# Routed experts on one core: row gathers in eight groups between GpSimd's weight splits, and the first tile's low part before the second split on VectorE

## The chip, the cores and the metric

The kernel runs on one core of a Trainium2 chip. A core has five engines that run side by side and meet only in semaphores: TensorE (PE), VectorE (DVE), ScalarE (ACT), GpSimd (POOL) and SyncE (SP), which here only issues DMAs. The metric is the device time of one execution in microseconds (us), as the median of several runs.

## The reference, cut to what matters

The program is two layers: cross attention and a gated feed-forward, then a state-space mixer and a mixture of experts. The change is in the mixture of experts alone, on 2048 tokens of 512 numbers, 16 experts, two for each token:

```python
logits = xt @ Wr.T + bias                      # 2048 x 16
probs = jax.nn.softmax(logits, axis=-1)
topk_val, topk_idx = jax.lax.top_k(probs, 2)
g = jnp.einsum('th,ehi->tei', xt, Wg)          # Wg, Wu: 16 x 512 x 256
u = jnp.einsum('th,ehi->tei', xt, Wu)
y = jnp.einsum('tei,eih->teh', jax.nn.silu(g) * u, Wd)   # Wd: 16 x 256 x 512
routed = jnp.einsum('tke,tk,teh->th', oh, w, y)
```

With these inputs and this routing the experts get 183, 203, 191, 89, 465, 257, 221, 103, 104, 332, 487, 937, 45, 11, 36 and 432 token slots.

## The kernel before, in words

The stages run one after the other; the last three are the router, the experts (`stage_experts`) and the sum (`stage_combine`). The router sorts the 4096 token slots by expert, and each expert's slots are padded to whole tiles of 128 rows. The number of tiles is fixed at 47 (`TILES`). From the counts above the experts 0 to 15 own 2, 2, 2, 1, 4, 3, 2, 1, 1, 3, 4, 8, 1, 1, 1 and 4 tiles, 40 in all; the seven tiles behind them are padding and use the last expert's weights. So tile 6 is the only one of expert 3, tiles 7 to 10 are expert 4's, 11 to 13 expert 5's, 14 and 15 expert 6's, tile 16 is expert 7's, tile 17 expert 8's, tiles 18 to 20 are expert 9's, 21 to 24 expert 10's, 25 to 32 expert 11's, and tile 35 is expert 14's.

`stage_experts` works a tile at a time. PE turns the tile's rows (`exp_x`, L2528), multiplies them with the expert's gate and up weights (`exp_g`), turns the hidden rows (`exp_h`) and multiplies them with the down weights (`exp_y_ps`). Every product is done in three passes with operands split in a high part (the fp32 number rounded by the cast) and a low part (the rest), `split_product`, L96. So the weights of an expert must be split before they can be used, and the tile's turned rows too: ACT writes their high part (`x_hi`, L2456), DVE their low part (`x_lo`, L2500).

Who does what, in which order:

- **SP** loads the raw weights of expert e: gate and up (`exp_raw`, two buffers, L2410) as soon as expert e-2 has been split, down (`exp_raw_down`, one buffer, L2413) as soon as expert e-1 has been split.
- **DVE** splits the weights of experts 0, 1 and 2 first (L2493, L2495), all three in a row, and only then takes the low part of tile 0's rows. Then it runs the loop over tiles.
- **POOL** first issues all 47 row gathers (L2421), one indirect DMA of 128 rows of 2 KB for each tile, in seven groups of 4, 4, 8, 8, 8, 8 and 7. A group has a semaphore of its own; after the issue of group g it waits for the landing of group g-1 and adds its size to `s_rows`. Behind the last gather it waits for the last group too. Only then does it split the weights of experts 3 to 15, one after the other (L2436, L2439: four instructions for an expert). Three experts' split weights fit (`WRING` is 3), so the split of expert e also waits until PE has done the last tile of expert e-3 (the wait on `s_y`).
- **ACT** copies a tile's gathered rows into a small buffer (`fetch`, L2451) two tiles ahead, when `s_rows` says that they are there. In its queue the copy for tile k+2 stands ahead of tile k's silu (L2474).
- **PE** waits before tile k's gate and up product for the split weights of its expert (`s_w`) and for the low part of the tile's rows (`s_xlo`).

Of the kernel before, what the change touches and what calls it, by code (L numbers as in the profile page):

```python
# [29 lines left out]
class Steps:  # L30
# [13 lines left out]
    def wait_apart(self, pace):  # L44
        wait_apart(self.eng, self.sem, self.base + self.n, pace)
# [1385 lines left out]
EXPERTS = 16  # L1431
# [585 lines left out]
WRING = 3  # L2017
# [320 lines left out]
def stage_experts(nc, xn, y, Wg, Wu, Wd, ident, plan):  # L2338
# [3 lines left out]
    IC = INNER // P  # L2342
    N_IN = KD * 2 * INNER
    N_ALL = N_IN + IC * DIM
    GROUPS = [4, 4] + [8] * 4 + [7]
    assert sum(GROUPS) == TILES
    with Scope(nc, "exp") as m:
        ident_sb = m.sb("ident", [P, P])
# [14 lines left out]
        s_raw, s_rawd = [m.sem(f"raw_in{i}") for i in range(2)], m.sem("raw_down_in")  # L2363
        s_gather = [m.sem(f"gathered{g}") for g in range(len(GROUPS))]
        s_rows = m.sem("rows_in")
# [12 lines left out]
        def pieces(e):  # L2378

            return ((raw[e % 2], slice(0, N_IN), s_raw[e % 2], 32 * (e // 2 + 1)),  # L2380
                    (raw_d, slice(N_IN, N_ALL), s_rawd, 16 * (e + 1)))
# [4 lines left out]
        def tiles(eng, step):  # L2386


            step(0, 0)
            pairs = (TILES - 3) // 2  # L2390
            with eng.Fori(0, pairs) as pair:
                step(pair * 2 + 1, 1)
                step(pair * 2 + 2, 0)
            for k in range(2 * pairs + 1, TILES + 1):
                step(k, k % 2)

        def known(k, test):

            return test(k) if isinstance(k, int) else True

        with m.block() as block:
            @block.sync
            def _(sp):
                sp.dma_start(ident_sb[:, :], ident).then_inc(s_id, 16)
                for e in range(EXPERTS):
                    if e >= 2:
                        sp.wait_ge(s_w, e - 1)
                    wi = raw[e % 2][:, 0:N_IN].rearrange("p (k g n) -> p k g n", k=KD, g=2)
                    for g, src in enumerate((Wg, Wu)):
                        sp.dma_start(wi[:, :, g, :], src[e].rearrange("(k p) n -> p k n", p=P)).then_inc(s_raw[e % 2], 16)  # L2410
                    if e:
                        sp.wait_ge(s_w, e)
                    sp.dma_start(raw_d[:, :].rearrange("p (k n) -> p k n", k=IC),  # L2413
                                 Wd[e].rearrange("(k p) n -> p k n", p=P)).then_inc(s_rawd, 16)

            @block.gpsimd
            def _(pool):
                k = 0
                for g, size in enumerate(GROUPS):
                    for _ in range(size):  # L2420
                        pool.indirect_dma_start(rows[:, k, :], None, xn,  # L2421
                                                bass.IndirectOffsetOnAxis(plan.source[:, k:k + 1], 0)
                                                ).then_inc(s_gather[g], 16)
                        k += 1
                    if g:
                        pool.wait_ge(s_gather[g - 1], 16 * GROUPS[g - 1])
                        pool.sem_inc(s_rows, GROUPS[g - 1])
                pool.wait_ge(s_gather[-1], 16 * GROUPS[-1])
                pool.sem_inc(s_rows, GROUPS[-1])
                for e in range(WRING, EXPERTS):  # L2430
                    end = pool.value_load(plan.ends[0:1, e - WRING:e - WRING + 1], min_val=0, max_val=TILES)
                    wait_apart(pool, s_y, end + 2, s_pace)
                    pool.wait_ge(s_w, e)
                    for n, (src, cols, sem, value) in enumerate(pieces(e)):
                        pool.wait_ge(sem, value)
                        pool.tensor_scalar(w[:, e % WRING, 0, cols], src[:, :], 1.0, 1.0, ALU.mult,  # L2436
                                           ALU.mult).then_inc(s_hi, 1)
                        pool.wait_ge(s_hi, 2 * (e - WRING) + n + 1)
                        pool.tensor_tensor(w[:, e % WRING, 1, cols], src[:, :], w[:, e % WRING, 0, cols].bitcast(F32),  # L2439
                                           ALU.subtract).then_inc(s_w if n else s_wpart, 1)  # L2440
                    pool.wait_ge(s_wpart, e + 1)

            @block.scalar
            def _(act):
# [40 lines left out]
            @block.vector  # L2485
            def _(dve):
                dve.sem_inc(s_xlo, 2)
                dve.sem_inc(s_h, 2)
                dve.sem_inc(s_hlo, 2)
                for e in range(WRING):  # L2490
                    for n, (src, cols, sem, value) in enumerate(pieces(e)):
                        dve.wait_ge(sem, value)
                        dve.tensor_copy(w[:, e, 0, cols], src[:, :]).then_inc(s_split, 1)  # L2493
                        dve.wait_ge(s_split, 2 * e + n + 1)
                        dve.tensor_tensor(w[:, e, 1, cols], src[:, :], w[:, e, 0, cols].bitcast(F32),  # L2495
                                          ALU.subtract).then_inc(s_w if n else s_wpart, 1)

                def x_lo(k, i):
                    dve.wait_ge(s_xhi, k + 1)
                    dve.tensor_tensor(xT[i][:, 1, :, :], ps_x[i][:, :, :], xT[i][:, 0, :, :].bitcast(F32),  # L2500
                                      ALU.subtract).then_inc(s_xlo, 1)

                x_lo(0, 0)

                def step(k, i):
                    if known(k, lambda k: k >= 1):
                        dve.wait_ge(s_hhi, k)
                        dve.tensor_tensor(hT[1 - i][:, 1, :, :], ps_h[1 - i][:, :, :], hT[1 - i][:, 0, :, :].bitcast(F32),
                                          ALU.subtract).then_inc(s_hlo, 1)
                    if known(k, lambda k: k + 1 < TILES):  # L2510
                        x_lo(k + 1, 1 - i)
                    if known(k, lambda k: k < TILES):
                        dve.wait_ge(s_silu, k + 1)
                        dve.tensor_tensor(hid[i][:, :], ps_g[i][:, 1, :], hid[i][:, :], ALU.mult).then_inc(s_h, 1)

                tiles(dve, step)
# [97 lines left out]
def build(nc, x, ctx_1024, L0_xattn_Wq, L0_xattn_Wk, L0_xattn_Wv, L0_xattn_Wo, L0_xattn_gq, L0_xattn_gk,  # L2614
# [20 lines left out]
    with Memory(nc, "residual") as r:  # L2635
# [14 lines left out]
        with Memory(nc, "normed2") as n:  # L2650
            normT2 = [n.sb(f"b{b}", [P, 2, KD, S], F32R) for b in range(B)]
            stage_norm(nc, "nrm2", xs, normT2, ident, rowsout=xrows)
            stage_shared_router(nc, xs, mixed, normT2, L1_ffn_sWg, L1_ffn_sWu, L1_ffn_sWd, L1_ffn_Wr, L1_ffn_bias, ident, iota, before, token, plan)

    stage_experts(nc, xrows, slots, L1_ffn_Wg, L1_ffn_Wu, L1_ffn_Wd, ident, plan)
    stage_combine(nc, mixed, slots, result, plan)
    decided.close()
# [30 lines left out]
```

## Time and profile before

| what | us |
| --- | --- |
| median of 3 runs (2758.46 to 2761.99) | 2759.77 |
| the profiled execution, its own time | 2749.03 |
| its span, first to last instruction | 2747.2 |
| stage of the experts in it, first gather to last product, about | 2371.5 to 2687 |

The profiled execution is one run on its own and was 10.7 us faster than the median of the three; its span leaves out 1.8 us around the instructions. Times in the trace count from the start of the span. The stage of the experts is 316 us of it.

### The profile page before, as it was taken

What the parts mean: (1) busy time and instruction counts of PE and PEld (TensorE: products, weight loads), DVE (VectorE), ACT (ScalarE), POOL (GpSimd) and SP (SyncE); (2) the same over time, 40 slices, a digit from 0 to 9 for tenths busy, and PEclk for the clock granted to TensorE, in tenths of its full rate; (3) what the DMA queues carried; (4) which work ended last, traced back from release to release, by engine and by line L of the source; (5) the groups of instructions that cost most, each with busy time, mean ns of one, the idle gap of its engine ahead of it and who ended that gap; (6) DMA issues with size and microseconds to landing.
All of it is one profiled execution on the core that took longest, in us unless ns stands there. A gap on an engine that the chain in (4) does not pass through costs nothing. (4 is left out here: it accounts for less than half of the span.)

```text
span 2747.2 us, 37910 instructions
## 1 busy us (share of the span) xinstructions
PE 2310.0 (84%) x10784; PEld 1774.8 (65%) x10785; DVE 1898.2 (69%) x3625; ACT 1235.3 (45%) x2129; POOL 1361.7 (50%) x1722
## 2 busy tenths in 40 slices
PE   3699999999999999998784898998998839459980
PEld 2687888878787878887533665665665426447770
DVE  6576777767677767776675989999999876412223
ACT  2353444544444444454483655655655412024440
POOL 0233333333243333332384888878988803478324
PEclk7799999999999999999886999999999958679995
DMA  7512232122322232220457555464665220565317
GB/s 276 206 62 101 85 109 86 62 90 85 109 85 76 76 109 85 85 77 28 142 202 237 176 180 184 173 197 151 205 195 158 86 89 16 201 201 175 130 54 256
DMA packets 136939, 363.84 MB, mean 132 GB/s; under 512 B 21280, under 2 KB 58912, under 8 KB 118560
## 3 DMA queue, kind: packets, MB, share of 16 engines
q1 hardware_dynamic: 123648, 328.36, 35.5%
q0 software_dynamic: 6320, 20.71, 2.4%
q10 hardware_dynamic: 6768, 12.32, 1.2%
q8 instruction: 94, 1.54, 0.2%
q14 instruction: 109, 0.89, 0.1%
HBM read 290.06 MB, written 71.30 MB: 132 GB/s over the span
## 5 line engine op out<-in xcount | busy, mean ns | idle before, releaser
L662 POOL TENSOR_SCALAR att_probs<-att_probs,att_recip 128x512 f32<-128x512 f32 x256 | 183.9, 722 | 402.5 <-DVE att_recip L743 398.1
L1837 POOL TENSOR_TENSOR mix_drive<-mix_du,mix_rows 128x512 f32<-128x512 f32 x256 | 326.5, 1282 | 61.4 <-DMA mix_rows<-bc_d 29.1
L585 ACT ACTIVATE att_probs<-att_s,att_bias,att_rq 128x512 f32<-128x512 f32 x256 | 199.9, 781 | 301.3 <-DVE att_bias L739 299.1
L1890 DVE TENSOR_TENSOR_SCAN mix_state<-mix_state,mix_drive 128x512 f32<-128x512 f32 x256 | 312.6, 1221 | 14.7 <-POOL mix_drive L1837 10.7
L1721 ACT ACTIVATE mix_state<-mix_delta,mix_a 128x512 f32<-128x512 f32 x256 | 176.7, 691 | 277.4 <-DVE mix_drive L1901 238.6
L1822 POOL TENSOR_TENSOR mix_y<-mix_y,mix_drive 128x512 f32<-128x512 f32 x180 | 230.6, 1281 | 79.0 <-DVE mix_drive L1901 79.0
L1630 PE MATMUL mix_down<-mix_wd,mix_hT 128*128 128x512 f32 x512 | 232.1, 596 | 8.7 <-DVE residual_x L1921 8.7
L738 DVE TENSOR_REDUCE att_nmax<-att_s 128x1 f32<-128x512 f32 x256 | 174.9, 683 | 64.7 <-PE att_s L101 64.7
L591 ACT CAST att_pT<-att_pt 128x512 fp32r<-128x512 f32 x256 | 143.4, 588 | 141.7 <-PE att_pt L442 137.6
L789 DVE TENSOR_TENSOR att_pT<-att_pt,att_pT 128x512 fp32r<-128x512 f32 x256 | 169.4, 682 | 44.6 <-ACT att_pT L591 44.2
L99 PE MATMUL att_w<-att_w_qkv,att_cx 128*128 128x256 f32 x512 | 161.9, 316 | 34.7 <-DVE att_w_qkv L725 26.7
L1630 PEld LDWEIGHTS mix_down<-mix_wd,mix_hT 128*128 128x128 f32 x512 | 97.4, 191 | 109.9 <-issue 95.8
L442 PE MATMUL att_pt<-att_ident,att_probs 128*128 128x128 f32 x1024 | 148.0, 281 | 12.0 <-DVE att_pT L789 10.8
L101 PE MATMUL att_w<-att_w_qkv,att_cx 128*128 128x256 f32 x512 | 155.5, 304 | 0.0
L100 PE MATMUL att_w<-att_w_qkv,att_cx 128*128 128x256 f32 x512 | 155.5, 304 | 0.0
L442 PEld LDWEIGHTS att_pt<-att_ident,att_probs 128*128 128x128 f32 x1024 | 117.4, 144 | 34.3 <-DVE att_pT L789 25.9
L99 PEld LDWEIGHTS att_w<-att_w_qkv,att_cx 128*128 128x128 f32 x512 | 108.1, 211 | 40.2 <-issue 37.8
L1901 DVE TENSOR_TENSOR mix_drive<-mix_state,mix_rows 128x512 f32<-128x512 f32 x180 | 124.5, 691 | 6.2
L99 PE MATMUL exp_g<-exp_w,exp_xT 128*128 x188 | 81.5, 434 | 54.6 <-POOL exp_w L2439 36.6
L99 PE MATMUL att_s<-att_kT,att_qT 128*128 128x512 f32 x256 | 107.5, 420 | 20.3 <-ACT att_probs L585 11.4
L669 POOL TENSOR_TENSOR att_work<-att_qguess 128x8 f32<-128x8 f32 x32 | 6.4, 199 | 236.9 <-DVE att_qguess L749 236.9
L600 ACT CAST att_oT<-att_o 128x512 fp32r<-128x512 f32 x64 | 37.6, 587 | 189.0 <-PE att_o L101 189.0
(359 smaller groups left out, 6789.5 us busy)
## 6 DMA issues: line engine op xcount, KB each, us to landing
att_xn<-normT SPq DMA_DIRECT2D x32, 2048.0 KB, 9.2
mix_gu<-guT SPq DMA_DIRECT2D x64, 1024.0 KB, 8.3
mix_rows<-bc_d SPq DMA_DIRECT2D x128, 256.0 KB, 5.0
guT<-att_ffnT SPq DMA_DIRECT2D x32, 512.0 KB, 3.4
mix_wd<-wdT SPq DMA_DIRECT2D x16, 1024.0 KB, 7.8
slots<-exp_y ACTq DMA_DIRECT2D x47, 256.0 KB, 2.0
normT<-nrm_outT SPq DMA_DIRECT2D x4, 2048.0 KB, 9.1
exp_raw<-in_L_ffn_Wg SPq DMA_DIRECT2D x16, 512.0 KB, 5.8
```

The source lines that it names most:

```text
L99: pe.matmul(out, lh, rh, start=start, stop=False)
L100: pe.matmul(out, lh, rl, start=False, stop=False)
L442: tr = pe.transpose(ps_pt[(b + n) % 2][:, t, :], probs[:, h * TB + t, k * P:(k + 1) * P], ident_sb[:, :])
L585: act.activation(probs[:, n, :], ps_s[n % 2][:, :], ACT.Exp, bias=bias[:, n:n + 1], scale=rq[:, n:n + 1], accum_out=sums[:, n:n + 1]).then ...
L662: pool.tensor_scalar(probs[:, n, :], probs[:, n, :], recip[:, n:n + 1], 1.0, ALU.mult, ALU.mult).then_inc(s_pn, 1)
L738: own.after(dve.tensor_reduce(nmax[:, n:n + 1], ps_s[n % 2][:, :], AX_X, ALU.max, negate=True))
L789: dve.tensor_tensor(pT[:, 1, k, :], ps_pt[(b + (TB + 1) * h + k) % 2][:, :, :].rearrange("p t n -> p (t n)"), pT[:, 0, k, :].bitcast(F32), ...
L1630: mm = pe.matmul(ps_y[:, :], hT[c % 2][:, k, tok], wd[c % 2][:, k, :], start=(k == 0), stop=(k == CHUNK - 1))
L1721: act.activation(state[q % BANKS][:, :], delta[i % DELTAS][:, :], ACT.Exp, scale=a[:, t, n:n + 1]).then_inc(s_decay, 1)
L1822: pool.tensor_tensor(out[:, :], out[:, :], drive[q % RING][:, :], ALU.add).then_inc(s_padd, 1)
L1837: pool.tensor_tensor(drive[q % RING][:, :], du[i % DUS][:, :], rows[g % ROWS][:, 0, :], ALU.mult).then_inc(s_drive, 1)
L1890: dve.tensor_tensor_scan(h[:, :], h[:, :], drive[q % RING][:, :], 0.0, ALU.mult, ALU.add).then_inc(s_scan, 1)
```

## The change

The gathers get eight groups of 2, 6, 8, 16, 4, 4, 4 and 3 tiles. POOL gathers group 0 and waits for it, waits until the raw weights of expert 0 have landed, gathers group 1 and waits for it, waits for the raw weights of expert 1, gathers group 2 and waits for it. Then it alternates: split expert 3, gather and await group 3, split expert 4, gather and await group 4, and so on to group 7 behind the split of expert 7. After that come the splits of experts 8 to 15. Every gather group is awaited before the next instruction of POOL. On DVE the low part of tile 0's rows moves from behind the splits of experts 0, 1 and 2 to right behind that of expert 0.

```diff
-    GROUPS = [4, 4] + [8] * 4 + [7]
+    GROUPS = [2, 6, 8, 16, 4, 4, 4, 3]
+    FIRST = 3
...
             def _(pool):
-                k = 0
-                for g, size in enumerate(GROUPS):
-                    for _ in range(size):
+                def gather(g):
+                    for k in range(sum(GROUPS[:g]), sum(GROUPS[:g + 1])):
                         pool.indirect_dma_start(rows[:, k, :], None, xn,
                                                 bass.IndirectOffsetOnAxis(plan.source[:, k:k + 1], 0)
                                                 ).then_inc(s_gather[g], 16)
-                        k += 1
-                    if g:
-                        pool.wait_ge(s_gather[g - 1], 16 * GROUPS[g - 1])
-                        pool.sem_inc(s_rows, GROUPS[g - 1])
-                pool.wait_ge(s_gather[-1], 16 * GROUPS[-1])
-                pool.sem_inc(s_rows, GROUPS[-1])
-                for e in range(WRING, EXPERTS):
+
+                def gathered(g):
+                    pool.wait_ge(s_gather[g], 16 * GROUPS[g])
+                    pool.sem_inc(s_rows, GROUPS[g])
+
+                def loaded(e):
+                    for _, _, sem, value in pieces(e):
+                        pool.wait_ge(sem, value)
+
+                def split(e):
...
+                gather(0)
+                gathered(0)
+                loaded(0)
+                gather(1)
+                gathered(1)
+                loaded(1)
+                gather(2)
+                gathered(2)
+                for e in range(WRING, EXPERTS):
+                    g = e - WRING + FIRST
+                    split(e)
+                    if g < len(GROUPS):
+                        gather(g)
+                        gathered(g)
...
-                for e in range(WRING):
+
+                def split_first(e):
...
+                split_first(0)
                 x_lo(0, 0)
+                for e in range(1, WRING):
+                    split_first(e)
```

**POOL, from the start of the stage.** Before, in the queue of POOL (L2421 is a gather, L2436 and L2439 are the four instructions of a split, L2431 and L92 its register work):

```order
L2416 UNCONDITIONAL_BRANCH
L2421 DMA exp_rows<-xrows,plan_source 128x512 x47
L2431 TENSOR_LOAD plan_ends
L2431 ISA x2
L92 REGISTER_ALU
L2436 TENSOR_SCALAR exp_w<-exp_raw 128x2048
L2439 TENSOR_TENSOR exp_w<-exp_raw,exp_w 128x2048
L2436 TENSOR_SCALAR exp_w<-exp_raw_down 128x1024
L2439 TENSOR_TENSOR exp_w<-exp_raw_down,exp_w 128x1024
```

All 47 gathers stand ahead of the first split. After the change the same stretch reads so, with the line numbers of the changed kernel (L2439 and L2442 are the split there, L2434 the register work):

```order
L2417 UNCONDITIONAL_BRANCH
L2421 DMA exp_rows<-xrows,plan_source 128x512 x16
L2434 TENSOR_LOAD plan_ends
L2434 ISA x2
L92 REGISTER_ALU
L2439 TENSOR_SCALAR exp_w<-exp_raw 128x2048
L2442 TENSOR_TENSOR exp_w<-exp_raw,exp_w 128x2048
L2439 TENSOR_SCALAR exp_w<-exp_raw_down 128x1024
L2442 TENSOR_TENSOR exp_w<-exp_raw_down,exp_w 128x1024
L2421 DMA exp_rows<-xrows,plan_source 128x512 x16
```

Sixteen gathers (groups 0, 1 and 2) stand ahead of the split of expert 3, sixteen (group 3) behind it; behind the splits of experts 4, 5, 6 and 7 stand 4, 4, 4 and 3. The waits for the landings don't show in such a list: there is one behind each group.

**DVE, from the start of the stage.** The difference in DVE's queue (L2500 before and L2519 after are the low part of a tile's rows):

```order
+L2512 CAST exp_w<-exp_raw 128x2048
+L2514 TENSOR_TENSOR exp_w<-exp_raw,exp_w 128x2048
+L2512 CAST exp_w<-exp_raw_down 128x1024
+L2514 TENSOR_TENSOR exp_w<-exp_raw_down,exp_w 128x1024
+L2519 TENSOR_TENSOR exp_xT<-exp_x,exp_xT 128x512
+L2512 CAST exp_w<-exp_raw 128x2048
```

Before, the first low part stood behind twelve split instructions, in one row with that of tile 1 (`L2500 TENSOR_TENSOR exp_xT<-exp_x,exp_xT 128x512 x2`); now it stands behind four. The low part of tile 1 stays behind all twelve.

## Rows read from the trace of the kernel before

**Rows 1.** The page: busy time, and PE, POOL and PE's clock in 40 slices.
```profile
PE 2310.0 (84%) x10784; PEld 1774.8 (65%) x10785; DVE 1898.2 (69%) x3625; ACT 1235.3 (45%) x2129; POOL 1361.7 (50%) x1722
...
PE   3699999999999999998784898998998839459980
...
POOL 0233333333243333332384888878988803478324
PEclk7799999999999999999886999999999958679995
```

**Rows 2.** Waits of the experts' stage: waiter <- releaser: total us, times, longest.
```profile
PE exp_g L99 <- POOL exp_w L2439: 36.6, 4, 24.3
PE exp_x L2528 <- ACT exp_row L2451: 18.8, 1, 18.8
PE exp_g L99 <- DVE exp_w L2495: 15.6, 1, 15.6
...
PE exp_g L99 <- DVE exp_xT L2500: 2.4, 1, 2.4
```

**Rows 3.** PE's timeline, where it restarts: start, duration, instruction [idle before <- releaser].
```profile
2401.27 0.79 PE L99 MATMUL exp_g<-exp_w,exp_xT 128*128 x1 [15.62 <-DVE exp_w L2495]
...
2456.57 0.79 PE L99 MATMUL exp_g<-exp_w,exp_xT 128*128 x1 [24.29 <-POOL exp_w L2439]
...
2466.66 0.50 PE L99 MATMUL exp_g<-exp_w,exp_xT 128*128 x1 [2.34 <-POOL exp_w L2439]
...
2526.89 0.79 PE L99 MATMUL exp_g<-exp_w,exp_xT 128*128 x1 [5.05 <-POOL exp_w L2439]
...
2620.66 0.79 PE L99 MATMUL exp_g<-exp_w,exp_xT 128*128 x1 [4.93 <-POOL exp_w L2439]
```

**Rows 4.** POOL's timeline, last gather and the splits of experts 3 to 10.
```profile
2437.79 0.95 POOL L2421 DMA_INDIRECT exp_rows<-xrows,plan_source  x1 [0.30 <-issue]
2446.26 1.90 POOL L2436 TENSOR_SCALAR exp_w<-exp_raw 128x2048 fp32r<-128x2048 f32 x1 [7.53 <-issue]
...
2456.26 1.90 POOL L2436 TENSOR_SCALAR exp_w<-exp_raw 128x2048 fp32r<-128x2048 f32 x1
...
2491.62 1.92 POOL L2436 TENSOR_SCALAR exp_w<-exp_raw 128x2048 fp32r<-128x2048 f32 x1 [5.04 <-PE exp_y_ps L101]
...
2506.30 1.91 POOL L2436 TENSOR_SCALAR exp_w<-exp_raw 128x2048 fp32r<-128x2048 f32 x1 [4.57 <-PE exp_y_ps L101]
...
2516.48 1.91 POOL L2436 TENSOR_SCALAR exp_w<-exp_raw 128x2048 fp32r<-128x2048 f32 x1
...
2526.59 1.90 POOL L2436 TENSOR_SCALAR exp_w<-exp_raw 128x2048 fp32r<-128x2048 f32 x1
```

**Rows 5.** ACT, silu of tiles 7 to 17: count, first and last start.
```profile
L2474 ACT ACTIVATE exp_hid<-exp_g x11: 384/385/386, 2469.8 to 2519.9; 128x256 f32<-128x256 f32 x11
```

**Rows 6.** DVE's timeline at the start: first split's ends, first low parts.
```profile
2376.88 1.23 DVE L2493 CAST exp_w<-exp_raw 128x2048 fp32r<-128x2048 f32 x1 [11.40 <-DMA exp_raw<-in_L_ffn_Wu]
...
2380.35 0.69 DVE L2493 CAST exp_w<-exp_raw_down 128x1024 fp32r<-128x1024 f32 x1
2381.07 1.23 DVE L2495 TENSOR_TENSOR exp_w<-exp_raw_down,exp_w 128x1024 fp32r<-128x1024 f32 x1
...
2400.33 1.28 DVE L2500 TENSOR_TENSOR exp_xT<-exp_x,exp_xT 128x512 fp32r<-128x512 f32 x2
```

**Rows 7.** ACT's timeline at the start: first two row copies, tile 0's high part.
```profile
2382.86 1.14 ACT L2451 COPY exp_row<-exp_rows 128x512 f32<-128x512 f32 x2 [26.28 <-POOLq L2427]
2384.70 0.58 ACT L2456 CAST exp_xT<-exp_x 128x512 fp32r<-128x512 f32 x1 [0.70 <-PE exp_x L2528]
```

**Rows 8.** Tile `exp_rows`, 2371 to 2374: issues in ns (min/median/max), and issue's start to landing.
```profile
L2421 POOL DMA_INDIRECT exp_rows<-xrows,plan_source x2: 958/1060/1162, 2371.5 to 2372.9; - x2
...
DMA to landing us min/median/max: 6.2/6.5/6.8
```

**Rows 9.** The same, 2376 to 2396, beside DVE's splits and the weight loads.
```profile
L2421 POOL DMA_INDIRECT exp_rows<-xrows,plan_source x12: 942/1540/2720, 2375.5 to 2395.5; - x12
...
DMA to landing us min/median/max: 6.3/7.0/8.0
```

**Rows 10.** The same, 2409 to 2429, no weight load under way.
```profile
L2421 POOL DMA_INDIRECT exp_rows<-xrows,plan_source x16: 944/946/949, 2409.0 to 2427.8; - x16
...
DMA to landing us min/median/max: 3.9/4.4/5.2
```

**Rows 11.** The same, all 47 gathers.
```profile
L2421 POOL DMA_INDIRECT exp_rows<-xrows,plan_source x47: 942/946/2720, 2371.5 to 2437.8; - x47
...
DMA to landing us min/median/max: 3.9/5.8/8.0
```

**Rows 12.** The same, the last seven (2430 to 2439).
```profile
L2421 POOL DMA_INDIRECT exp_rows<-xrows,plan_source x7: 942/946/947, 2430.3 to 2437.8; - x7
...
DMA to landing us min/median/max: 4.5/6.4/7.3
```

## The prediction

> **What bounds the kernel now.** I read the page first. PE is busy 84% of the span, but the 35th and 36th digits of its row are 4 and 5, while POOL's are 4 and 7 [rows 1]. A slice is 68.7 us, so these two are where the experts' stage begins, and the change touches that stretch alone. Then I asked who waits for whom in the experts' stage. PE waits 36.6 us for POOL's weight splits, in four waits, one of them 24.3 us, and 15.6 us once for DVE's splits (on top of 18.8 us for the first rows) [rows 2]. The timeline of PE places them: tile 0's product starts at 2401.27, tile 6 (expert 3) is ready 24.29 us before it starts at 2456.57, tile 7 (expert 4) starts at 2466.66, tile 18 (expert 9) at 2526.89 after 5.05 us, tile 35 (expert 14) at 2620.66 after 4.93 us [rows 3]. All of the last four are released by a split on POOL. So up to tile 18 the stage is a race between POOL's queue and PE, and POOL is late three times (24.29, 2.34 and 5.05 us). Between the waits PE needs 5.0 us for a tile: eleven silus in 50.1 us, ten periods [rows 5].
>
> POOL's timeline tells why. The last of 47 gathers is issued at 2437.79, the first split starts at 2446.26, and from there a split takes 10.0 us (2446.26 to 2456.26) to 10.1 us (2516.48 to 2526.59) [rows 4]. In between POOL waited 9.6 us (5.04 + 4.57) for PE to give a slot of the weight ring back. The split of expert 9 ends at about 2526.6, and PE takes up tile 18 at 2526.89.
>
> **Behind tile 18 nothing changes in kind.** The later splits (10 to 15) are paced by PE through the weight ring, or run right behind each other as before. So tile 18's start is the point to forecast: whatever it shifts, the end of the kernel shifts.
>
> **The change on DVE and at the start.** Tile 0's low part now stands behind the first split alone, which ends at 2382.3 (2381.07 + 1.23) [rows 6]. It also needs the high part. Now the first group is two gathers, and they land up to 6.8 us after an issue at about 2372.9, so at 2379.7 [rows 8]. From ACT's row copy to the end of the high part are 2.4 us (2382.86 to 2385.28) [rows 7]: ready at 2382.1. The low part costs 0.65 us (half of the 1.28) [rows 6], so tile 0's product starts at about 2383.3, 18 us earlier than 2401.27. That is not passed on. Tile 1's low part and tile 0's hidden product stay behind the splits of experts 1 and 2 on DVE, and ACT's silu of tile 0 stands behind the copy of tile 2's rows, which are in group 1. DVE ended its splits at 2400.3 [rows 6]; with fewer gathers beside the weight loads I put that at 2397, so tile 1 gains some 3 to 8 us, and PE has gone cold twice (a restart shows a first product of 0.79 us, or of 0.50 after a short wait [rows 3]). It turns out not to matter, since PE will wait for POOL again at tile 7.
>
> **The change on POOL, worked out in order.** The instructions are the same, 47 gathers and 13 splits; what is added is that POOL stands still behind every group until it has landed. I call L the time from the last issue's start to its landing. The one place that shows such a standstill is the 7.53 us before the first split, with a landing of 7.3 us [rows 4, 12]: so the standstill is L + 0.25 (less the issue of 0.95, plus 1.2 for the semaphore and the register work of the split). A group of n gathers behind a split costs n x 1.25 (0.946 of issue [rows 10] and 0.30 before it [rows 4]) + L + 0.25.
>
> - Group 0 and expert 0's weights: landed at 2379.7 as above. POOL goes on at 2379.8.
> - Group 1, six gathers beside DVE's splits: 6 x 1.84 (1540 + 300 ns [rows 9]) = 11.0, to 2390.8, landed 5.5 later (7.0 - 1.5 [rows 9]) at 2396.3. Expert 1's weights are there long before.
> - Group 2, eight gathers: 8 x 1.25 = 10.0, about 1 more where they meet the last split on DVE, and L + 0.25 = 6.05 with the median L of 5.8 [rows 11]. The split of expert 3 starts at 2413; it may, since tile 1 is done at about 2411.
> - It ends at 2423.1, before PE is ready for tile 6 (some 2424 to 2428). The wait of 24.29 us is gone.
> - Group 3, sixteen gathers: 20.0 + 4.65, L being 4.4 as in the stretch with no load under way [rows 10]: 24.7. Split of expert 4: 10.1. It ends at 2457.9. PE is ready for tile 7 at about 2431 and waits 27 us; it starts 8.5 us earlier than before.
> - Groups 4, 5 and 6, four gathers each, and a split behind each: 5.0 + 6.05 + 10.1 = 21.15. SP issues three weight loads just as a split ends, so I take the median L of 5.8. Splits 5, 6 and 7 end at 2479.0, 2500.2 and 2521.3. Tiles 11, 14 and 16 need them at 2479, 2495 and 2511: PE waits 0, 5 and 10 us.
> - Group 7, three gathers: 3.75 + 6.05 + 10.1 = 19.9. Split 8 ends at 2541.2, tile 17 needs it at 2528.
> - Split 9 ends at 2551.3. Tile 18 is ready at 2548 and waits again.
>
> The sum: 2413 + (24.7 + 3 x 11.05 + 9.8) + 7 x 10.1 = 2551.3, against 2526.6 before: **24.7 us later**. Or as a balance: 31 gathers (38.75 us) and five standstills (28.85) now lie between the splits of experts 3 and 9, where the row of before has 9.6 us of waits for the ring; against that the first split starts 33.3 us earlier (2413 for 2446.3). 38.75 + 28.85 - 9.6 - 33.3 = 24.7. Further restarts of PE at low clock cost nothing, since PE waits for POOL behind them anyway, and tile 18 starts cold in both.
>
> The profiled execution would take 2749.03 + 24.7 = 2773.7 by this; on the median of the runs, which is 10.7 higher, it is 2759.77 + 24.7 = 2784.5 us.
>
> **Bounds of the unknown.** The landing of a small group behind a split, beside three weight loads, is not in the trace. From below 3.9 us, the shortest of all [rows 11]; from above 8.0, the longest. I take 5.8 because the groups meet loads for part of their time only. At 3.9 everywhere the sum falls by 5 x 1.9 + 0.5 = 10.0, and if group 1 issued undisturbed by another 3.4: +11. At 7.3, the most of the last seven gathers [rows 12], it rises by 5 x 1.5 + 2.9 = 10.4: +35; at 8.0 by 14.6: +39. The two last groups fetch the padding tiles, and it was these that landed late, 6.4 in the median [rows 12], which speaks for the upper half.
>
> The trace shows 3.9 us and more for a gather of 256 KB [rows 11]. The Trainium skill, "DMA: Bandwidth & Descriptors", section "Anatomy of one DMA", fits a DMA issued from GpSimd with about 2.0 us plus the bytes over 436 GB/s, which would be 2.6 us here. By that the five standstills at 5.8 and the one at 4.4 would be 17.8 us shorter and the kernel 7 us slower instead of 25. The rows speak against it, for its figure is below the shortest of 47.
>
> **The rivals.**
> - *Short standstills* (chance 0.15). The gathers of a small group run nearly alone, L is about 3.9 or less. For it: 3.9 to 5.2 us in the quiet stretch [rows 10]. Against it: the loads that each split's end releases. The time is some 2771.
> - *Long standstills* (0.12). L of 7.3 to 8.0 behind every split, loads and padding together: 2795 to 2799.
> - *The gathers go out beside the split* (0.08). POOL's sequencer runs ahead of the engine, so that a group's issue begins under the last instructions of the split before it. For it: splits follow each other without a gap, although a register load stands between them [rows 4]. Against it: the gather is a busy row of 0.95 us on POOL itself [rows 10]. It could hide at most the last 3.4 us (1.05 + 2.39) of five splits, 17 us: 2767 to 2768.
> - *Faster: the standstills cost nothing* (0.03). If the awaited landings were over when POOL asks, the six standstills of groups 2 to 7 (34.9 us) would vanish from the sum, and what is left is the earlier start of the splits: 24.7 - 34.9 = -10.2, 2749.6. The point from which it decides is where these six together cost less than 10.2 us, 1.7 each. The 7.53 us [rows 4] speak against it, and that no landing is under 3.9 [rows 11].
> - *The front gain alone shows* (0.02): tile 0's 18 us reach the end. Then POOL would have to keep up to tile 18, needed by PE at about 2495 without waits; even bare splits and issues take it to 2523.
>
> **How the numbers follow.** The forecast has 0.60: 2784.5, between 2776 and 2792. The rivals' ends are at +11 and +39; I leave out the outermost and take 2770 to 2796. What a measurement of this kernel can tell from no change is 0.2%, 5.5 us. Slower by more is the forecast, the long and nearly all of the short standstills and of the issue beside the split: 0.91 (0.60 + 0.12 + 0.14 + 0.05). Within 0.2% needs both small mechanisms, or the smaller of them at its best: 0.05. Faster are the last two: 0.04, with what is left of the others.
>
> **What would show it.** In the trace of the changed kernel: tile 0's product near 2383; no wait, or a short one, at tile 6; one of 20 to 30 us at tile 7, released by POOL; further ones at tiles 14, 16, 17 and 18, growing to 10 us and more; on POOL, idle times of 4 to 8 us behind the last gather of each group; no more waits of the splits 7 and 8 for PE; the split of expert 9 ending near 2551. Wrong it is if the standstills are under 3 us, if gathers overlap splits, or if PE does not wait for POOL at tiles 16 to 18.

## The result, and the profile after

| | before | after |
| --- | --- | --- |
| median of 8 runs each, same chip, us | 2757.53 (2752.10 to 2761.99) | 2776.66 (2769.53 to 2783.11) |
| ratio, with its 95% interval | | 1.0069 [1.0053, 1.0085] |
| profiled execution, own time | 2749.03 | 2783.11 |
| its span | 2747.2 | 2781.3 |

The change makes the kernel 19 us slower; the interval holds 15 to 23 us. One run of `late_gathers` below took 5346 us, nearly twice the rest, and is left out of its median and ratio as a slow one.

The page of the kernel after, the lines that answer to [rows 1]:

```profile
PE 2319.7 (83%) x10784; PEld 1781.4 (64%) x10785; DVE 1898.7 (68%) x3625; ACT 1237.5 (44%) x2129; POOL 1359.4 (49%) x1722
...
PE   3699999999999999998865997998988659565981
...
POOL 0233333333233333332575878988888512467324
PEclk7799999999999999999877999999999869787995
```

Busy times are those of before to within half a per cent on every engine; nothing is computed twice. What changed is digits 35 to 37: PE 5, 6, 5 where it was 4, 5, 9, and POOL 4, 6, 7 where it was 4, 7, 8. POOL spreads the same work over a longer stretch, and PE stays half idle for one slice more.

The waits of the experts' stage of the kernel after (2371 to 2725; waiter <- releaser: total us, times, longest), PE's against [rows 2]:

```profile
PE exp_g L99 <- POOL exp_w L2442: 48.0, 7, 13.5
PE exp_h L2567 <- DVE exp_hid L2536: 26.8, 2, 14.8
...
PE exp_x L2550 <- ACT exp_row L2469: 15.9, 1, 15.9
```

The waits for POOL went from four (36.6 us) to seven (48.0 us). PE's timeline of the kernel after shows where, against [rows 3] (start, duration, instruction [idle before <- releaser]):

```profile
2390.02 0.79 PE L99 MATMUL exp_g<-exp_w,exp_xT 128*128 x1 [0.88 <-DVE exp_w L2514]
...
2453.46 0.69 PE L2567 MATMUL exp_h<-exp_ident,exp_hid 128*128 128x128 f32 x2 [14.79 <-DVE exp_hid L2536]
...
2463.45 0.79 PE L99 MATMUL exp_g<-exp_w,exp_xT 128*128 x1 [8.45 <-POOL exp_w L2442]
...
2506.16 0.67 PE L99 MATMUL exp_g<-exp_w,exp_xT 128*128 x1 [3.44 <-POOL exp_w L2442]
...
2528.57 0.79 PE L99 MATMUL exp_g<-exp_w,exp_xT 128*128 x1 [10.91 <-POOL exp_w L2442]
...
2549.48 0.79 PE L99 MATMUL exp_g<-exp_w,exp_xT 128*128 x1 [13.51 <-POOL exp_w L2442]
...
2559.61 0.49 PE L99 MATMUL exp_g<-exp_w,exp_xT 128*128 x1 [2.94 <-POOL exp_w L2442]
```

These are tile 0, the long hole of tiles 6 and 7 in two pieces, and tiles 14, 16, 17 and 18. POOL's timeline of the kernel after, against [rows 4] (L2421 a gather, L2439 the first instruction of a split; the brackets are POOL's standstills):

```profile
2377.84 1.16 POOL L2421 DMA_INDIRECT exp_rows<-xrows,plan_source  x1 [13.04 <-POOLq L75]
...
2386.98 1.14 POOL L2421 DMA_INDIRECT exp_rows<-xrows,plan_source  x1 [6.74 <-DMA exp_rows<-xrows,plan_source]
...
2403.76 0.97 POOL L2421 DMA_INDIRECT exp_rows<-xrows,plan_source  x1 [6.41 <-DMA exp_raw<-in_L_ffn_Wu]
...
2419.39 1.92 POOL L2439 TENSOR_SCALAR exp_w<-exp_raw 128x2048 fp32r<-128x2048 f32 x1 [5.27 <-PE exp_y_ps L101]
...
2453.16 1.90 POOL L2439 TENSOR_SCALAR exp_w<-exp_raw 128x2048 fp32r<-128x2048 f32 x1 [3.65 <-DMA mix_work<-u_d]
...
2474.55 1.91 POOL L2439 TENSOR_SCALAR exp_w<-exp_raw 128x2048 fp32r<-128x2048 f32 x1 [6.51 <-DMA exp_rows<-xrows,plan_source]
...
2495.72 1.91 POOL L2439 TENSOR_SCALAR exp_w<-exp_raw 128x2048 fp32r<-128x2048 f32 x1 [6.09 <-DMA exp_rows<-xrows,plan_source]
...
2518.26 1.90 POOL L2439 TENSOR_SCALAR exp_w<-exp_raw 128x2048 fp32r<-128x2048 f32 x1 [7.53 <-DMA exp_rows<-xrows,plan_source]
...
2539.19 1.90 POOL L2439 TENSOR_SCALAR exp_w<-exp_raw 128x2048 fp32r<-128x2048 f32 x1 [7.31 <-DMA exp_rows<-xrows,plan_source]
2549.19 1.90 POOL L2439 TENSOR_SCALAR exp_w<-exp_raw 128x2048 fp32r<-128x2048 f32 x1
2559.30 1.92 POOL L2439 TENSOR_SCALAR exp_w<-exp_raw 128x2048 fp32r<-128x2048 f32 x1
```

The splits of experts 3 to 10 start here. The one of expert 9 is over when that of expert 10 starts, at 2559.30, and tile 18 starts at 2559.61. The releaser named in a bracket is the last event seen; "mix_work<-u_d" before the split of expert 4 can only be a wrong name for a gather's landing, since the mixer is long over. This profile lacks about a fifth of the landing records of the stage (1859 of 2288), so where it names a DMA, the name isn't sure. The same holds for `early16`, `pad_rows`, `before_again` and `late_gathers`; the other eight profiles have all 2288.

The stages ahead of the experts are untouched but not equally long in each execution: the first gather is issued between 2366 and 2380 in the profiles of this study. So from here on times of the stage count **from the first gather**:

| profile | split 3 starts | tile 0 | tile 6 | tile 7 | tile 18 | end of stage |
| --- | --- | --- | --- | --- | --- | --- |
| before | 74.8 | 29.8 | 85.1 | 95.2 | 155.4 | 320.4 |
| forecast for after | 41.5 | 11.8 | | 86.4 | 180.1 | |
| after | 41.6 | 12.2 | 56.5 | 85.6 | 181.8 | 348.4 |

"End of stage" is the first gather of the sum; from there to the end of the kernel it is 55 to 56 us in every profile.

### The profile page after: what moved, and what is told of

Read it like the earlier page. It is cut to its first block and busy times, and to the rows that moved or that the text cites. A ratio compares the mean times of both kernels' runs of the same rounds, so it can differ in the third digit from the quotient of the medians.

```text
span 2781.3 us, 37913 instructions
## 1 busy us (share of the span) xinstructions
PE 2319.7 (83%) x10784; PEld 1781.4 (64%) x10785; DVE 1898.7 (68%) x3625; ACT 1237.5 (44%) x2129; POOL 1359.4 (49%) x1722
## 5 line engine op out<-in xcount | busy, mean ns | idle before, releaser
L442 PE MATMUL att_pt<-att_ident,att_probs 128*128 128x128 f32 x1024 | 148.6, 281 | 12.1 <-DVE att_pT L789 10.9
```

The source lines that it names most:

```text
L442: tr = pe.transpose(ps_pt[(b + n) % 2][:, t, :], probs[:, h * TB + t, k * P:(k + 1) * P], ident_sb[:, :])
```

## The experiments

The theory is that tile 18 starts when POOL's queue up to the split of expert 9 is done, and that nothing ahead of it counts. Rivals: the move on DVE costs or gains something; the standstills are not what costs; the length is one of memory contention.

### The same kernel again, and each half of the change alone

`again` is the changed kernel unchanged. `dve_only` is the kernel before with only `split_first(0)`, `x_lo(0, 0)`, `split_first(1)`, `split_first(2)` in that order. `pool_only` is the reverse:

```diff
-                split_first(0)
-                x_lo(0, 0)
-                for e in range(1, WRING):
+                for e in range(WRING):
                     split_first(e)
+                x_lo(0, 0)
```

> The changed kernel as it is, once more, for a second profile. From the first gather to tile 18's product the profile of the changed kernel took 181.8 us, that of before 155.4 us: 26.4 more, while the medians of the runs differ by 19.1. If the loss sits in POOL's queue alone (forecast), this stretch is 178 to 184 us again and whatever differs in the end comes from stretches that the change does not touch. If the landings scatter from run to run, the stretch itself moves by several us, and its mean lies near 155.4 + 19 = 174.5. Time against before: slower by 15 to 24 us.

> The kernel before with the move on VectorE alone (tile 0's low part behind the first split); GpSimd as before. Theory (the race is lost on POOL): tile 0's product starts near 2386 instead of 2401, but the split of expert 3 still ends near 2456 and tile 18 starts where it did; the time is that of before within 2 us. Rival (the early start is passed on): some 5 to 15 us faster than before.

> The changed kernel with the low part of tile 0 back behind all three of VectorE's splits. In the changed kernel the split of expert 3 was released by tile 1's last product (a wait of 5.3 us for PE). Theory: with tile 0 late, tile 1 is done some 5 us later, the split of expert 3 starts that much later, and since everything on POOL up to tile 18 follows it back to back, the kernel is about 5 us slower than the changed one: 22 to 32 us slower than before. Rival (the move on VectorE is without effect in this kernel too): as slow as the changed kernel, within 2 us.

| | median us | ratio to before, 95% | tile 0 | tile 6 | tile 7 | tile 18 | end of stage |
| --- | --- | --- | --- | --- | --- | --- | --- |
| again | 2774.65 | 1.0083 [1.0060, 1.0106] | 12.5 | 57.3 | 87.4 | 184.4 | 346.9 |
| dve_only | 2753.24 | 1.0005 [0.9985, 1.0024] | 14.4 | 83.4 | 93.4 | 157.6 | 324.8 |
| pool_only | 2776.94 | 1.0101 [1.0073, 1.0129] | 27.6 | 59.4 | 88.1 | 185.1 | 347.6 |

(Before, measured beside them: 2753.63 us.) **The whole loss is POOL's queue.** In `dve_only` tile 0 is 15 us earlier, and PE still waits for POOL at tile 6, 25.6 us long; tile 18 stands where POOL's queue lets it. The waits of the experts' stage, PE's, in `dve_only`:

```profile
PE exp_g L99 <- POOL exp_w L2439: 42.4, 5, 25.6
```

`again` has tile 18 at 184.4, just outside the 178 to 184 expected: the stretch moves by 2 to 3 us between the two profiles.

I had expected `pool_only` to be some 5 us above `again`, since tile 1 would be done later and the split of expert 3 waits for it. It is 2 us above in the median, with overlapping intervals. PE's and POOL's timelines of `pool_only`:

```profile
2394.20 0.79 PE L99 MATMUL exp_g<-exp_w,exp_xT 128*128 x1 [16.39 <-DVE exp_w L2514]
```

```profile
2410.65 1.92 POOL L2439 TENSOR_SCALAR exp_w<-exp_raw 128x2048 fp32r<-128x2048 f32 x1 [6.77 <-PE exp_y_ps L101]
```

The split starts 44.1 us after the first gather, right behind the end of tile 1 at 43.8. In `again` tile 1 ends at 40.9, but there the last gather of group 2 lands at 42.2 and comes last, and the split starts at 43.5. In after tile 1 comes last again, at 40.6, and the split starts at 41.6. So the late low part costs 2.9 to 3.2 us at the end of tile 1. Against `again`, where the landing hides most of that, 0.6 us are left at the split; against after it is 2.5. On the kernel's time this can't be told from nothing.

### The same queue without the standstills

`mid_wait` has the same gathers and splits in the same order. Only the waits for the landing of groups 3 to 7 are moved, to between the two halves of the next split:

```diff
-                def split(e):
+                def split(e, landed=None):
...
                     for n, (src, cols, sem, value) in enumerate(pieces(e)):
+                        if n and landed is not None:
+                            gathered(landed)
                         pool.wait_ge(sem, value)
...
-                    split(e)
+                    split(e, g - 1 if FIRST < g <= len(GROUPS) else None)
                     if g < len(GROUPS):
                         gather(g)
-                        gathered(g)
```

> The changed kernel, but groups 3 to 7 are issued behind their splits without waiting for the landing; the wait and the count of the rows stand in the middle of the next split, 6.5 us later. Takes away the five standstills alone (27.4 + 3.65 us of idle time in the profile of the changed kernel, less 1 us of register work each), keeps all issues. Theory (issues and standstills both cost in full): about 27 us faster than the changed kernel, that is 3 to 10 us faster than before. Rival (the gathers' issue alone already makes PE wait, the standstills are hidden behind weight loads or PE): at most 10 us faster than the changed kernel, still slower than before.

It took 2750.90 us, 0.9992 [0.9972, 1.0012] of before: 24 us below `again`, and not the 3 to 10 us below before that I had expected. Tile 18 starts at 153.5. Five standstills are gone (31.1 us in the profile of after); in their place the split of expert 8 waits 2.0 us and that of expert 9 0.6 us for the ring, and one landing, that of group 6, still holds POOL for 1.1 us in the middle of a split. 31.1 - 2.6 - 1.1 = 27.4, the first split starts 1.1 us earlier, and tile 18 is 28.3 us earlier than in after. POOL's timeline of `mid_wait`, last gather of group 3 and the split of expert 4, and the middle of the split of expert 7:

```profile
2449.01 0.95 POOL L2421 DMA_INDIRECT exp_rows<-xrows,plan_source  x1 [0.30 <-issue]
2449.98 1.91 POOL L2441 TENSOR_SCALAR exp_w<-exp_raw 128x2048 fp32r<-128x2048 f32 x1
2451.98 4.49 POOL L2444 TENSOR_TENSOR exp_w<-exp_raw,exp_w 128x2048 fp32r<-128x2048 f32 x1
2456.44 1.04 POOL L2441 TENSOR_SCALAR exp_w<-exp_raw_down 128x1024 fp32r<-128x1024 f32 x1
...
2502.58 1.04 POOL L2441 TENSOR_SCALAR exp_w<-exp_raw_down 128x1024 fp32r<-128x1024 f32 x1 [1.07 <-DMA exp_rows<-xrows,plan_source]
```

The split follows 0.02 us behind the last issue. The landing is asked for between its second and third instruction, and there is no wait there: what had cost 3.65 us is over by then. The same holds for the other groups, but for the 1.07 us behind group 6, four gathers of padding. So **the loss is the standstills**: the gathers still stand between the same splits, and the memory sees the same traffic, yet the kernel is as fast as before. The mixing with its earlier first split gives nothing either.

### What the early split is worth

`early16` puts the sixteen gathers of group 3 ahead of the split of expert 3 (one group of 24):

```diff
-    GROUPS = [2, 6, 8, 16, 4, 4, 4, 3]
+    GROUPS = [2, 6, 24, 4, 4, 4, 3]
```

> The changed kernel with the group of sixteen joined to that of eight: 24 gathers behind group 1, then splits with groups of 4, 4, 4 and 3 behind the first four. Same issues and splits on POOL ahead of the split of expert 9, one standstill less (3.65 us), but the splits of experts 3 and 4 end 20 us and 1 us later or earlier. Theory (only the sum on POOL up to the split of expert 9 counts): PE waits at tile 6 instead of tile 7 and tile 18 starts 3 to 8 us earlier than in the changed kernel. Rival (that the split of expert 3 comes early is worth something in the end): slower than the changed kernel.

It took 2777.16 us, 1.0062 [1.0038, 1.0087] (before, measured beside it: 2755.51). The split of expert 3 starts at 63.2 instead of 41.6, tile 6 at 80.9 instead of 56.5, and tile 18 at 182.0 instead of 181.8. Twenty-two microseconds of head start for expert 3 show nowhere: what counts is the length of POOL's queue. The 3 to 8 us that I had expected from the standstill saved (3.65 us) did not come: group 2 starts 2.5 us later than in after, and the four standstills that remain are 2.1 us longer in sum (29.5 for 27.4).

### The padding tiles' gathers

In the profile of after, the two groups that hold the padding tiles stand still longest, 7.53 and 7.31 us. All rows of a padding tile are fetched from one place. `pad_rows` gives them the rows of tiles 0 to 6 instead:

```diff
-                                                bass.IndirectOffsetOnAxis(plan.source[:, k:k + 1], 0)
+                                                bass.IndirectOffsetOnAxis(plan.source[:, k % 40:k % 40 + 1], 0)
```

> The changed kernel, but the seven padding tiles (40 to 46, 128 times the same row each) gather the rows of tiles 0 to 6 instead, whose products nobody reads. In the changed kernel the standstill was 7.5 and 7.3 us behind the two groups of padding, 6.5 and 6.1 us behind the two before them, 3.65 us behind the sixteen. If reading one row over and over is what makes the padding land late, these two fall to 5.5 to 6.5 us and the kernel gains 2 to 4 us; if it is the weight loads that start with each group, they stay at 7.3 to 7.5 us.

POOL's timeline of `pad_rows`, the splits of experts 7 and 8:

```profile
2505.73 1.92 POOL L2439 TENSOR_SCALAR exp_w<-exp_raw 128x2048 fp32r<-128x2048 f32 x1 [5.45 <-DMA exp_rows<-xrows,plan_source]
...
2525.78 1.90 POOL L2439 TENSOR_SCALAR exp_w<-exp_raw 128x2048 fp32r<-128x2048 f32 x1 [6.42 <-DMA exp_rows<-xrows,plan_source]
```

5.45 and 6.42 us, against 7.53 and 7.31 in after, 7.76 and 7.57 in `again`, 8.05 and 7.42 in `pool_only`. The others stay (3.67, 6.91, 6.52). The landings of group 7 say the same, first in `again`, then in `pad_rows`:

```profile
DMA to landing us min/median/max: 6.3/7.1/7.6
```

```profile
DMA to landing us min/median/max: 6.2/6.4/6.7
```

So a small group whose gathers read one row 128 times each is waited for 1 to 2.6 us longer than one that reads different rows. Tile 18 starts at 178.1, but on the time this is small: 2774.03 us, 1.0068 [1.0050, 1.0087], not to be told from after's.

### The kernel before once more

> The kernel before as it is, for a second profile. Its first one, 2749 us, was faster than the median of its runs. If the experts' stage is the same in every run, the stretch from the first gather to the first gather of the sum takes 320 us as in the first profile, and only the stages ahead of it scatter. The other kernel with the same GpSimd queue took 325 us, so 320 to 325 us is what I expect.

`before_again` took 2758.02 us (1.0008 [0.9993, 1.0023]), yet its profile has tile 18 at 160.6 and the stage's end at 327.4, seven later than the first profile of before and outside the 320 to 325 expected. Five of the seven are there at tile 18, and ahead of it stands one hole. The waits of PE and ACT in the experts' stage of `before_again`:

```profile
ACT exp_y L2478 <- DMA mix_du<-du_d: 15.8, 1, 15.8
...
PE exp_y_ps L99 <- issue: 16.4, 1, 16.4
```

ACT is 15.8 us late with a copy (again the name of the releaser is wrong), and PE is out for 16.4 us before a down product. The hole of 14.79 us at tile 6 in the profile of after is of this kind: PE waits for DVE's hidden product, and that for ACT's silu. It did not come back in `again`. `early16` has one of 20.2 us and `pad_rows` one of 14.3. With the new queue it lies ahead of a wait for POOL and costs nothing.

The hole may belong to the recording. All four profiles that have it are among the five that lack a fifth of their landing records, and most of the missing ones fall in the 50 us around it; none of the eight complete profiles has one. No run tests this, so `before_again` is a weak witness for what the stage of the kernel before takes.

### A version that beats both

If only POOL's queue up to the split of expert 9 counts, gathers should go behind it. `late_gathers` issues sixteen gathers, then the splits of experts 3 to 6 back to back, and each later group only as its tiles come near, with the wait in the middle of the next split as in `mid_wait`:

```diff
-    GROUPS = [2, 6, 8, 16, 4, 4, 4, 3]
+    GROUPS = [2, 6, 8, 4, 4, 4, 4, 8, 7]
+    BEHIND = {6: 3, 7: 4, 9: 5, 10: 6, 11: 7, 12: 8}
...
+                last = None
                 for e in range(WRING, EXPERTS):
-                    g = e - WRING + FIRST
-                    split(e)
-                    if g < len(GROUPS):
-                        gather(g)
-                        gathered(g)
+                    split(e, last)
+                    last = BEHIND.get(e)
+                    if last is not None:
+                        gather(last)
```

> A schedule made from the theory: 16 gathers, then the splits of experts 3 to 6 back to back, groups of 4, 4, 4, 4, 8 and 7 gathers behind the splits of experts 6, 7, 9, 10, 11 and 12, each awaited in the middle of the next split. Only four gathers lie before the split that PE needs at tile 16, eight before that of tile 18. Theory: tile 18 starts about 122 us behind the first gather (155 before), the kernel is about 33 us faster than before, ratio 0.986 to 0.990. Rival (PE or the stores of y become the bound once POOL keeps up, at 5.4 us a tile instead of 5.0): tile 18 at 130 us or later, less than 25 us faster.

The median of five runs is 2739.22 us, the ratio to before 0.9939 [0.9919, 0.9959]: faster than before by 17 us, but tile 18 starts at 130.3 where the theory had about 122. POOL is hardly to blame any more (PE waits 12.9 us for it in the whole stage). What is late is ACT. Its timeline in `late_gathers`, copies of a result into the buffer `y`, each followed by its store:

```profile
2441.19 0.59 ACT L2498 COPY exp_y<-exp_y_ps 128x512 f32<-128x512 f32 x1 [1.07 <-DMA slots<-exp_y]
...
2452.99 0.59 ACT L2498 COPY exp_y<-exp_y_ps 128x512 f32<-128x512 f32 x1 [2.93 <-DMA slots<-exp_y]
...
2465.70 0.59 ACT L2498 COPY exp_y<-exp_y_ps 128x512 f32<-128x512 f32 x1 [3.45 <-DMA slots<-exp_y]
```

In 26.5 us of waits, ten of them, the copy by this profile stands until the last store has landed (31.2 us in nine waits in the complete profile of `late_again`, below), and ACT's high parts for the next products are queued behind it. To try this, `late_y_rows` drops the buffer and copies the result into the tile's own gathered rows, which nobody reads any more; `before_y_rows` has that edit on the kernel before, and `late_again` repeats `late_gathers`:

```diff
-                        wait_apart(act, s_st, 16 * k, s_pace)
-                        act.copy(yout[:, :], ps_y[1 - i][:, :]).then_inc(s_yout, 1)
+                        act.copy(rows[:, k - 1, :], ps_y[1 - i][:, :]).then_inc(s_yout, 1)
                         act.wait_ge(s_yout, k + 2)
-                        act.dma_start(y[bass.ds((k - 1) * P, P), :], yout[:, :]).then_inc(s_st, 16)
+                        act.dma_start(y[bass.ds((k - 1) * P, P), :], rows[:, k - 1, :]).then_inc(s_st, 16)
```

> late_gathers, and the product y of a tile is copied into the place of the tile's gathered rows, which nobody reads any more, and stored from there, instead of through one buffer that is free only when the store before has landed. In late_gathers ACT's copy of y waited 26.5 us in ten waits for stores, and a tile took 5.8 us between tiles 7 and 35 outside the split waits where PE alone takes 4.7. Theory (once POOL keeps up, the single buffer for y is the bound while gathers and weight loads share the DMA queues): the experts' stage is 15 to 30 us shorter than in late_gathers, the kernel 30 to 45 us faster than before. Rival (the stage is paced by the weight ring and POOL's splits): within 6 us of late_gathers.

> The kernel before with the same change of y's buffer alone. Its copy of y waited 16.9 us for stores in nine waits, and its second profile showed one such wait of 15.8 us. Theory: before tile 18 POOL's splits set the time, so only what lies behind counts, some 5.3 instead of 4.8 us a tile for about ten tiles: 3 to 8 us faster than before. If stores were the bound all along: 15 us or more.

> late_gathers once more on this chip, for its comparison with late_y_rows: 0.6% faster than before as measured, that is 11 to 23 us; tile 18 at 126 to 132 us behind the first gather.

| | median us | ratio to before, 95% | tile 18 | end of stage |
| --- | --- | --- | --- | --- |
| late_y_rows | 2717.39 | 0.9865 [0.9844, 0.9887] | 122.3 | 285.3 |
| before_y_rows | 2747.13 | 0.9971 [0.9956, 0.9986] | 154.9 | 316.5 |
| late_again | 2736.18 | 0.9919 [0.9899, 0.9939] | 129.6 | 304.5 |

(Before, measured beside them: 2753.82 us.) Tile 18 now starts at 122.3, as the queue alone would have it. The waits of ACT and PE in `late_again`, then that of PE in `late_y_rows`, in the experts' stage:

```profile
ACT exp_y L2498 <- DMA slots<-exp_y: 31.2, 9, 6.1
...
PE exp_y_ps L99 <- DVE exp_hT L2532: 14.3, 7, 3.9
PE exp_g L99 <- POOL exp_w L2444: 13.9, 4, 5.2
```

```profile
PE exp_g L99 <- POOL exp_w L2443: 14.9, 5, 5.1
```

A store of one tile's result lands after 2.0 us when alone and after up to 9.7 us beside gathers and weight loads in `late_y_rows`, where nobody waits for it. In the kernel before the same edit is worth 0.3%, 7 us; with the late gathers it is worth 19 us (2736.18 less 2717.39). That fits the reading that the moved gathers stand beside the stores and the one buffer hands the late landings on to ACT and PE; the edit shows that the buffer is the cause, and that the gathers make the stores late is argued from the landings alone. `late_y_rows` is 1.3% faster than before and, by the two ratios, 2% faster than after.

## Why the prediction was right

The forecast was 2784.5 us, in a range of 2770 to 2796. Measured: 2776.66. Step by step, by the text above:

- **What bounds.** Tile 18 starts 0.31 us behind the end of expert 9's split, as in the kernel before. Behind it little changed: from its start to the end of the stage 165.0 us before, 166.6 after, 162.5 in `again`. That low-clock restarts ahead of tile 18 cost nothing fits: in after the granted clock was 0.81 in the 96 us up to tile 18 and 0.95 behind it; before, 0.88 and 0.97. The windows of the kernel after, then of before (us, busy of PE, PEld, DVE, ACT, POOL; PEclk, DMA share, GB/s):

```profile
2463.20:2559.30 96.10, 63.09 (x264) 50.06 (x264) 16.96 (x33) 25.80 (x55) 63.80 (x35) 0.81 0.46 153
2559.30:2724.00 164.70, 148.26 (x694) 118.58 (x694) 43.34 (x85) 66.00 (x141) 59.43 (x24) 0.95 0.29 99
```

```profile
2446.20:2526.60 80.40, 61.70 (x288) 49.69 (x288) 18.50 (x36) 28.20 (x60) 69.11 (x29) 0.88 0.48 157
2526.60:2691.50 164.90, 148.09 (x694) 118.35 (x694) 43.32 (x85) 65.79 (x141) 59.34 (x24) 0.97 0.29 99
```

- **The front.** Tile 0 at 12.2 (forecast 11.8), and it is not passed on: shown by `dve_only`.
- **Group 0 and 1.** Group 1 begins at 9.1, not 8.3, group 2 at 25.9, not 24.8. The prediction let POOL go on 0.1 us behind a landing. In `again`, whose landings are all on record, group 0 lands at 8.35 (forecast 8.2), and group 1 begins 0.84 us behind it; group 1 lands at 26.55, and group 2 begins again 0.84 us behind it. The weight load that the bracket in after names is not the cause: in `again` expert 1's weights are there at 16.0.
- **The first early split** starts at 41.6 (forecast 41.5), but in this profile for another reason than written: not the landing of group 2 comes last, but PE's end of tile 1 (5.27 us of wait, released by `exp_y_ps`). In `again` it is the landing, as written, and the split starts at 43.5. The prediction had the two within 2 us of each other; that it hit the tenth is luck.
- **Standstills.** Forecast 4.65, three times 6.05 and 6.05, in sum 28.85. Measured 3.65, 6.51, 6.09, 7.53 and 7.31, in sum 31.1. The sum is nearly right because errors cancel. In `again` the last gathers of the five groups land after 3.6, 6.7, 6.3, 7.7 and 7.6 us, where the prediction took 4.4 and four times 5.8; but the next split starts 0.95 to 1.0 us behind the landing, where it took 1.2. The last two groups fetch padding and stood still 1.3 to 1.5 us longer than forecast; the prediction named that as speaking for the upper half, and `pad_rows` shows why.
- **The sum.** From the start of expert 3's split to the end of expert 9's, 138.3 us forecast, 139.9 measured. Tile 18: 180.1 and 181.8. Against the profile of before that is +26.4 us, forecast +24.7. `mid_wait` shows that with five standstills gone nothing is left of the loss.
- **PE's waits.** Tiles 11, 14, 16 and 17: 0, 3.4, 10.9 and 13.5 us, for 0, 5, 10 and 13 (2541 less 2528). At tile 7 one wait of 27 us was forecast; in `again` it is one of 24.8, in the profile of after 14.8 and 8.5 with PE's hole at tile 6 between.
- **The rivals.** Short standstills: only the one behind the sixteen gathers is (3.65 us), the other four are 6.1 to 7.5 us. Gathers beside the split: no row shows one, each gather stands behind its split's last instruction. Costless standstills: this is `mid_wait`, which takes five of the six out. By the prediction's sum that is 24.7 - 28.85 = -4, 4 us ahead of before; 3.7 us of waits come back, and tile 18 stands 1.9 us ahead of before's profile. In the kernel's time it is no gain at all (0.9992).
- **The page's figure.** By the Trainium skill, "DMA: Bandwidth & Descriptors", section "Anatomy of one DMA", a gather of this size would be there after an estimated 2.6 us and the kernel 7 us slower. The trace doesn't agree: no standstill is under 3.65 us, with an issue of 0.95 us ahead of it, the shortest landing of the 47 in `again` is 3.3 us, and the loss is 19 us.

**What was off is the size on the median**, 7.8 us. 2.2 of it is the base: the three runs of before shown had 2759.77, the eight have 2757.53. 5.6 is the step "2749.03 + 24.7, and on the median the same 24.7", set against 19.1 us between the medians. This may be in part the noise of one comparison: the three timed comparisons of the new queue say 19 (15 to 23), 23 (17 to 29) and 28 us (20 to 36). The profiles don't settle it either. Three with POOL's old queue and one buffer (before, `before_again`, `dve_only`) end the stage at 320.4, 327.4 and 324.8, in the mean 324.2; three with the new queue (after, `again`, `pool_only`) at 348.4, 346.9 and 347.6, in the mean 347.6. That is 23.4 us; the two complete ones on either side alone say 24.7 (322.6 and 347.3). So 24.7 may be as good as 19, and why the first comparison is the smallest is open.

## What to carry to other kernels

An engine that issues DMAs and also computes should not wait for a landing where its next instruction doesn't need it: the wait costs what is left of the flight (here 4 to 8 us, five times), while the same waits half a split later cost 1.1 us in all. Before moving work ahead, find the one instruction downstream that collects all waits (here the split of the ninth expert) and add up what stands ahead of it in that queue: a head start for anything sooner, 22 us of it here, is worth nothing, and moving work behind that point is worth nearly its full length at that instruction, once nothing else binds: from `mid_wait` to `late_y_rows` 23 gathers (28.75 us) go behind it, and tile 18 starts 31.2 us earlier. With the one buffer still there it was 23.9. Then look at what had been hidden by the old bound, here a single buffer that a store must leave.

## What the runs showed of the hardware that was not expected

- An indirect gather of 128 rows of 2 KB that all come from one row lands later than one of different rows: the standstill behind the two padding groups is 7.3 to 8.4 us in four profiles, and 5.5 and 6.4 us with different rows. It isn't the only thing that counts: in `early16` the standstill behind tiles 32 to 35, of whose 512 slots 133 are in use, is 7.9 us, and 6.5 to 6.9 behind the same tiles in four other profiles.
- A store of 256 KB that lands in 2.0 us alone takes up to 9.7 us beside gathers and weight loads (`late_y_rows`).
- Four of the thirteen profiles (`before_again`, after, `early16`, `pad_rows`) have a hole of 14.3 to 20.2 us on PE that ends 64 to 76 us into the stage, behind an instruction of ACT that starts 10 to 19 us after its last visible condition. Both queues have it. Its cause is open, and since it stands only in profiles that lack landing records, it may come from the recording.
